# Node phase: the order of TensorE's z products and of the turning of the second norm's rows

## The reference

```python
gi = agg @ W_ih.T + b_ih
gh = h @ W_hh.T + b_hh
r = jax.nn.sigmoid(i_r + h_r)
z = jax.nn.sigmoid(i_z + h_z)
n = jnp.tanh(i_n + r * h_n)
h_new = (1.0 - z) * n + z * h
bn = gamma * (h_new - run_mean) * jax.lax.rsqrt(run_var + BN_EPS) + beta
return h + bn
...
x = x + _L0_gnn_ref(_layernorm(x, axis=-1), edge_index, edge_attr_128, ...)
x = x + _L0_ffn_ref(_layernorm(x, axis=-1)[None], L0_ffn_Wg, ...)[0]
```

## Time and profile before

| | before |
|---|---|
| median of 3 runs (lowest to highest) | 1388.26 us (1388.04 to 1388.4) |
| the profiled execution, its own time | 1388.83 us |
| its span, first to last instruction | 1387.0 us |
| PE busy / PEld busy | 1333.9 us (96%) / 1103.0 us (80%) |
| DVE / ACT / POOL busy | 944.5 us (68%) / 756.6 us (55%) / 830.5 us (60%) |
| mean granted TensorE clock | 0.990 |
| tiles in the node phase | 79, the last turning starts at 1368.53 us |

### The profile page before, as it was taken

One profiled execution on the slowest core, in us unless ns is written; L12 is line 12 of the kernel. 1 busy time (PEld: TensorE's weight loads), 2 busy tenths in 40 slices (PEclk: granted clock), 3 DMA queues, 4 the chain that ended last, 5 costly groups with the idle time before them and its releaser, 6 DMA issues. The chain is left out here.

```text
span 1387.0 us, 22825 instructions
## 1 busy us (share of the span) xinstructions
PE 1333.9 (96%) x6398; PEld 1103.0 (80%) x6398; DVE 944.5 (68%) x2115; ACT 756.6 (55%) x1744; POOL 830.5 (60%) x1119
## 2 busy tenths in 40 slices
PE   4899999999969999999999999999999999999996
PEld 3678888887758888888888888888888888888884
DVE  3585443333467777777777777777777777777775
ACT  3341323211266666666666666666666666666652
POOL 3210241302467777777777777777777777777771
PEclk9999999999989999999999999999999999999998
DMA  8213435335633433333343333333343343433320
GB/s 318 71 46 114 152 129 173 113 113 200 217 114 119 137 116 133 122 127 133 116 136 121 129 127 123 132 125 129 117 133 124 126 136 114 136 121 129 126 102 31
DMA packets 62864, 179.58 MB, mean 129 GB/s; under 512 B 9328, under 2 KB 9968, under 8 KB 62704
## 3 DMA queue, kind: packets, MB, share of 16 engines
q1 hardware_dynamic: 46912, 99.20, 21.0%
q0 software_dynamic: 15920, 79.97, 17.3%
HBM read 141.86 MB, written 37.29 MB: 129 GB/s over the span
## 5 line engine op out<-in xcount | busy, mean ns | idle before, releaser
L1549 PE MATMUL bank<-whh_hi,x_hi 128*128 128x512 f32 x948 | 383.9, 405 | 11.3 <-DVE x L1495 10.4
L1549 PE MATMUL bank<-whh_lo,x_hi 128*128 128x512 f32 x948 | 375.5, 396 | 0.0
L1549 PE MATMUL bank<-whh_hi,x_lo 128*128 128x512 f32 x948 | 375.0, 396 | 0.0
L1549 PEld LDWEIGHTS bank<-whh_hi,x_hi 128*128 128x128 f32 x948 | 178.7, 188 | 52.2 <-DVE x L1495 10.8
L1549 PEld LDWEIGHTS bank<-whh_hi,x_lo 128*128 128x128 f32 x948 | 178.7, 188 | 44.4
L1549 PEld LDWEIGHTS bank<-whh_lo,x_hi 128*128 128x128 f32 x948 | 178.9, 189 | 39.1
L1295 POOL TENSOR_TENSOR rstd<-var_eps,minus_half 128x1 f32<-128x1 f32 x158 | 90.6, 574 | 153.3 <-DVE var_eps L479 153.3
L1286 POOL DMA_INDIRECT gates<-gates_in,slot_at x79 | 85.2, 1078 | 59.9 <-issue 45.7
L1455 DVE TENSOR_TENSOR h_lo<-bank,h_hi 128x512 fp32r<-128x512 f32 x79 | 54.6, 691 | 84.5 <-ACT h_hi L1390 84.5
L1340 POOL TENSOR_TENSOR n_pre<-r_hn,gates 128x512 f32<-128x512 f32 x79 | 102.8, 1302 | 13.4 <-POOL r_hn L1336 13.2
L1348 POOL TENSOR_TENSOR h_n<-h,n_gate 128x512 f32<-128x512 f32 x79 | 104.0, 1316 | 1.8 <-ACT n_gate L1404 1.8
(11 more groups left out here) (184 smaller groups left out, 3098.6 us busy)
## 6 DMA issues: line engine op xcount, KB each, us to landing
xt<-in_x SPq DMA_DIRECT2D x79, 256.0 KB, 2.8
x_lo_raw<-in_x_cols SPq DMA_DIRECT2D x79, 256.0 KB, 2.7
out<-y SPq DMA_DIRECT2D x79, 256.0 KB, 2.0
gates_in<-g_out SPq DMA_DIRECT2D x16, 768.0 KB, 3.8
wih_lo_raw<-in_wih_t SPq DMA_DIRECT2D x4, 768.0 KB, 12.4
whh_rows<-in_whh SPq DMA_DIRECT2D x4, 768.0 KB
whh_lo_raw<-in_whh_t SPq DMA_DIRECT2D x4, 768.0 KB, 8.4
gates_in<-late_out SPq DMA_DIRECT2D x6, 256.0 KB, 6.7
```

Source lines behind the costliest of these rows:

```text
L1549: last = pe.matmul(to[0:R, :], a[:, s, k * R:(k + 1) * R], w[:, k, q * D:(q + 1) * D], start=n == 0, stop=n == 3 * DK - 1)
```

## The change

In TensorE's body the turning of `h2` goes in front of all z products instead of between their halves. The wait for `x1_done` moves along with z's first matmul. The number of instructions, the waits on every instruction group, and the streams of the other engines stay as they are.

```diff
                 if p.has(0):
                     s = p.slot(0)
                     pe.wait_ge(x_lo_done, t + 1)
                     wait_from(pe, r_pre_done, t - 1)
                     gate(s, b_r[s], 0).then_inc(r_prod, 1)
                     wait_from(pe, hn_done, t)
                     gate(s, b_n, 2).then_inc(n_prod, 1)
-                if p.has(0):
-                    wait_from(pe, x1_done, t)
-                    gate(p.slot(0), b_z, 1, 0, 2)
                 if p.has(-1):
                     pe.wait_ge(h2_done, t)
                     wait_from(pe, h2_lo_done, t - 1)
                     turn(pe, b_th2, h2[:, p.slot(-1), :], DK).then_inc(h2_turned, 1)
                 if p.has(0):
-                    gate(p.slot(0), b_z, 1, 2, DK).then_inc(z_prod, 1)
+                    wait_from(pe, x1_done, t)
+                    gate(p.slot(0), b_z, 1).then_inc(z_prod, 1)
```

## The result

| | before | changed |
|---|---|---|
| median (lowest to highest), 4 runs each | 1388.33 us (1388.04 to 1389.19) | 1409.53 us (1407.97 to 1410.08) |
| ratio, 95% interval | 1 | 1.015 (1.0132 to 1.0167) |
| the profiled execution / its span | 1388.83 / 1387.0 us | 1410.08 / 1408.3 us |
| PE busy, DVE busy | 1333.9, 944.5 us | 1347.1, 938.6 us |

What follows compares the result with a forecast made beforehand. PE bounds the node phase; with h2's cover spent, it waits in each tile. 76 x 0.25 = 19.0, plus 1.9 at the start and 1.4 at the end, is 22.3 us: 1410.6 us, range 1402 to 1418.

Steps and rivals of the forecast that it cites:

- the cover of h2: From h2's end on ScalarE (L1381) to its turning on PE: mean 1.23 us, against 1.40 us of matmuls moved.
- The wait comes back in each tile: PE's first expert products start the chain to the next h2, so PE waits in each tile, not just once.
- The ring: h2 ready, turning, twelve of z, turning of hid, first expert products, L1474, chain, next h2: 12.68 us against PE's 12.43.
- 0.25 us for a tile: Loss per tile: 0.28 (0.17 missing cover, 0.05 release, 0.06 weight load), less small returns from side inputs; range 0.20 to 0.33.
- The exposed weight load: At h2's turning, after a wait, the weight load is no longer made ahead: 0.06 us; a whole load is 107 ns.
- Start and end: First tile's z behind its turning: 1.9 us lost (1.2 to 2.7, by the clock's rise); last tile's z later: 1.4 us.
- The wait did not die out: Rival: h2's chain keeps a 12.32 us pace, PE waits only a few times, 1391 us; chance 0.06.
- the swing of the clock after short pauses: Rival: PE's pauses put one tile in ten at 1.2 GHz, 83 us more, near 1490 us; chance 0.02.
- The first expert products gained nothing: Rival: a wait for h2_lo before them falls away, up to 0.10 us a tile, 1403 us; chance 0.08.
- The two signs of being wrong: L1474's start to h2's end below 6.9 us, or first expert product behind hid's turning by clearly less than 0.25 us.
- PE's busy share from 450 to 1350 us: Sign expected in the profile: PE's share of that stretch near 98%, at clock 1.00.
- VectorE's idle time before L1474: Sign expected in the profile: VectorE idle longer than 0.68 us before L1474, its step behind the first expert products.

Runs made afterwards that it cites:

- The two lengthened kernels: One more VectorE instruction behind L1474, adding 0.0 to its 296 columns: 1449.83 us in the changed kernel, 1390.23 us in the kernel before.

## Why the prediction was right

- **PE's work bounds, and the cover of h2 is the only thing that the change spends.** Right. The six matmuls moved, 1.40 us, stand against a mean cover of 1.23 (1.16 over all tiles, since it grows in the first ten). Three moved cost nothing, five next to nothing, six 0.23 us a tile.
- **The wait comes back in each tile, since h2 hangs on PE's own first expert products.** Right, and this was the step that decided between 1391 and 1411 us. The two lengthened kernels show it: 0.51 us more between L1474 and L1487 cost 0.53 us a tile in the changed order and nothing a tile in the old one.
- **The ring, 12.68 us.** Measured 12.675. That it agrees to the last digit is in part luck: 12.68 was added up for one period, and the mean of the four was 12.71, from which the forecast then took 0.03 off. Its parts, for the whole loop: turning to L1474 5.45 (5.38 and 0.06 for the exposed load, forecast), L1474 to h2's end 7.17, release 0.05.
- **0.25 us for a tile.** Measured 0.231. From the 0.28 two pieces are missing. From L1474 to h2's end it is 7.11, 7.11, 7.18 and 7.29 us in the loop's four periods, where it was 7.20, 7.11, 7.18 and 7.30: 0.025 came back on the average, where 0.03 was taken off. It came in one period alone (0.09 us), where h_n had held L1487 back. The other piece named, h2 starting 0.11 us behind its shift, is still there (0.11 in both kernels). The other 0.025 was not foreseen: from the turning to L1474 it was 3.98 or 3.99 and 4.04 us by turns before, and is 5.45 in all periods now, not 5.45 and 5.50.
- **The exposed weight load.** 0.06 us, as at the second tile: from the turning to z's first matmul it is 0.41 us here as well. The whole load of 0.11, which the prediction took from the Trainium skill, "TensorE: Matmul & The Clock Gate", section "LDWEIGHTS (loading the stationary operand)", as the other bound, would have been 0.05 a tile more, 4 us over the whole; this trace shows no more than 0.06 of it.
- **Start and end.** 1.9 forecast, 2.27 measured (its ends were 1.2 and 2.7); 1.4 forecast, 1.41 measured. 1.9 was a choice between these two, and the high end's condition is what came: the granted clock from 396 to 412 us fell from 0.84 to 0.75, and z's first eight matmuls behind the first turning ran 0.43 us apart or more, at 1.2 GHz, until about 404.1 us. The twelve took 4.59 us (400.37 to 404.96), as reckoned; the six of before took 1.85 and not 1.6, and the turning started 0.12 us earlier than before, so less than 2.7 was lost.
- **The rivals.** The wait did not die out. The 12.32 us for a tile, from which this rival was drawn, were not the pace of the chain behind L1474: in the third to the eleventh tile of the kernel before, L1487 starts 0.10 us behind the end of h_n each time, while its distance from L1474 shrinks from 2.14 to 1.21 us. So GpSimd's h_n held h2 there, and the ring took over when h_n had come early enough. From 450 to 1350 us the clock stayed at 1.00, the 2.4 GHz level, with a pause in each tile, so the swing of the clock after short pauses, which the prediction cited from the Trainium skill, "TensorE: Matmul & The Clock Gate", section "A second HAM failure mode: psum-queue depth-cycling", is shown by no run here. The first expert products gained nothing: from the turning of h2 to the first of them it was 2.10 us on the average, with 1.40 and 0.06 it would be 3.56, and 3.55 was measured. The two signs of being wrong stayed away: L1474 to the end of h2 is 7.17 us on the average, not below 6.9, and the first expert product follows the turning of hid by 0.25.
- **What was wrong among the signs.** PE's busy share from 450 to 1350 us is 99.6% and not near 98%: the ends of matmuls are modelled, and they cover most of a pause of 0.2 us. VectorE's idle time before L1474 did not grow (55.9 us in 79 waits, 56.6 before); the additional idle time came ahead of L1462, z_pre, since h2_lo is done earlier and z isn't (117.4 us, 78 times). Neither was a term of the sum.

One thing stays open. With three of z ahead, the step is 12.414 and not 12.443: every second period of the kernel before is 0.06 us longer than in that kernel, between the turning of h2 and the end of the first expert products. It is the same unevenness that is gone in the changed kernel, too. What makes it was not tried; with 76 x 0.03 = 2.2 us it pays back what start and end cost with three ahead.

## What to carry to other kernels

Before you move work of the bounding engine behind one of its waits, measure the cover of that wait (from the maker's end to the waiting instruction) and compare it with the work moved; what is too much comes back in each iteration if the maker itself hangs on this engine's output. Follow the maker back until you reach the bounding engine or a free-running source: that answers whether a stall is paid once or in every tile. And if one path of a ring is shortened, look at the side inputs first, since here the next one was 0.15 us behind, and it passed through the bounding engine at another place (n's products).

## What the hardware showed that was not expected

- With the turning of hid first, its first weight load starts 0.23 us after the end of GpSimd's L1322, which it waits for, where that of h2 starts 0.05 us after ScalarE's L1381. Both are waits of PE for another engine. It is not so for all that GpSimd releases: h2 on ScalarE starts 0.03 us after GpSimd's L1298, and L1487 on VectorE 0.10 us after h_n. The profile doesn't tell whether the signal of L1322 is late or its recorded end too early.
- A pause of 0.2 us is next to invisible in PE's busy time, and shows in the idle time of the weight loads and in the distance between starts.
- The three transposes of 128x128 of hid cost 0.33 us of PE between a 512-wide matmul and four more transposes, and also ahead of the 296-wide ones (0.25 and 0.08), so putting two turnings side by side saves nothing.
- A pause of PE in each tile did not bring the clock down in these runs: from 450 to 1350 us it was 1.00 with pauses of 0.13 to 0.32 us in each tile of 12.7 us, and also in the changed kernel with the additional VectorE instruction, where a tile took 13.2 us.
